# A new order of work on every engine in the attention phase of a cross-attention and FFN kernel

## What is computed

```python
def attn(q, k, v, wq, wk, wv, wo):          # q = layernorm(x), k = v = ctx
    Q, K, V = (split_heads(a @ w) for a, w in ((q, wq), (k, wk), (v, wv)))
    corr = irfft(rfft(Q) * conj(rfft(K)))   # over the 128 places
    top_vals, top_idx = top_k(corr, 4)
    w = softmax(top_vals)
    out = sum(w[i] * roll(V, top_idx[i]) for i in range(4))   # roll within a head's 16
    return merge_heads(out) @ wo

x = x + attn(layernorm(x), ctx, ctx, wq, wk, wv, wo)
x = x + ffn(layernorm(x), W_in, b_in, W_out, b_out)   # gelu, int8 weights, 16-bit activations
```

## Time and profile before

| | us |
|---|---|
| median of 3 runs | 1145.84 (1144.47 to 1146.34) |
| the profiled execution | 1144.86 |
| its span, first to last instruction | 1143.1 |
| TensorE busy | 1024.5 (90%) |
| VectorE busy | 970.0 (85%) |
| ScalarE busy | 942.9 (82%) |
| GpSimd busy | 518.1 (45%), nearly all of it in the attention phase |

### The profile page before, as it was taken

The page is one execution under the profiler, slowest core; times in us unless marked ns, Lnnn a source line. Parts: engine busy times, 40 slices in busy tenths (PEclk is TensorE's granted clock), DMA queues, the critical chain, the costliest instruction groups (busy, mean ns, idle before and its releaser), DMA issues. The chain is left out here.

```text
span 1143.1 us, 30275 instructions
## 1 busy us (share of the span) xinstructions
PE 1024.5 (90%) x9870; PEld 759.9 (66%) x9870; DVE 970.0 (85%) x2838; ACT 942.9 (82%) x1805; POOL 518.1 (45%) x742
## 2 busy tenths in 40 slices
PE   6888888888888888888888789999999999999998
PEld 5677666766667667667766654444444588888887
DVE  4777778777887777787777999999999899999998
ACT  4677877787788888777887778888888899999996
POOL 5887777777777777787777650000000100000000
PEclk9999999999999999999999999999999999999999
DMA  5443333223332433332333129999999999999995
GB/s 157 135 135 120 110 112 112 90 98 112 112 102 91 125 112 112 112 104 99 98 111 112 39 86 321 304 309 307 309 308 301 373 342 346 362 354 359 357 346 211
DMA packets 133783, 222.94 MB, mean 195 GB/s; under 512 B 72480, under 2 KB 76192, under 8 KB 129568
## 3 DMA queue, kind: packets, MB, share of 16 engines
q1 hardware_dynamic: 132272, 220.12, 56.8%
q10 hardware_dynamic: 1392, 1.31, 0.4%
HBM read 121.26 MB, written 83.89 MB: 179 GB/s over the span
## 5 line engine op out<-in xcount | busy, mean ns | idle before, releaser
L657 PE MATMUL sums<-wout,arena 128*128 128x256 f16 x2048 | 229.7, 273 | 1.2 <-DVE arena L1555 1.2
L657 PEld LDWEIGHTS sums<-wout,arena 128*128 128x128 f16 x2048 | 197.0, 98 | 32.4 <-DVE arena L1548 7.3
L1555 DVE SCALAR_TENSOR_TENSOR arena<-arena,wout_rel 128x512 f16<-128x512 int16 x256 | 180.2, 745 | 2.0 <-ACT arena L932 0.9
L477 PE MATMUL sums<-store_x,arena 128*128 128x256 f16 x768 | 94.1, 272 | 93.8 <-ACT arena L677 93.8
L748 ACT ACTIVATE arena<-arena 32x128 f32<-32x128 f32 x256 | 78.5, 307 | 118.5 <-DVE arena L1243 116.2
L1250 DVE SCALAR_TENSOR_TENSOR arena<-sums,arena 128x256 f32<-128x256 f32 x128 | 56.1, 480 | 130.5 <-ACT arena L716 130.5
L477 PEld LDWEIGHTS sums<-store_x,arena 128*128 128x128 f16 x768 | 70.7, 97 | 116.8 <-issue 108.9
L1021 POOL TENSOR_TENSOR arena<-arena 128x512 f16<-128x512 f32 x64 | 74.3, 1160 | 94.6 <-ACT arena L677 94.6
L626 PE MATMUL sums<-arena,win 128*128 128x512 f16 x512 | 115.9, 379 | 0.7 <-DVE arena L1500 0.7
L626 PE MATMUL bank<-arena,win 128*128 128x512 f16 x512 | 115.7, 379 | 0.0
L1519 DVE TENSOR_REDUCE hmax_all<-arena 128x1 f32<-128x1024 f32 x96 | 111.2, 1210 | 2.9 <-ACT arena L889 2.9
(11 more groups left out here) (152 smaller groups left out, 2428.2 us busy)
## 6 DMA issues: line engine op xcount, KB each, us to landing
hidden_scratch<-arena SPq DMA_DIRECT2D x32, 1536.0 KB, 5.6
arena<-hidden_scratch SPq DMA_DIRECT2D x64, 768.0 KB, 6.7
arena<-in_ctx_turned SPq DMA_DIRECT2D x64, 256.0 KB, 4.1
arena<-in_x_turned SPq DMA_DIRECT2D x64, 256.0 KB, 3.0
arena<-in_x SPq DMA_DIRECT2D x64, 256.0 KB, 3.9
x_scratch<-arena SPq DMA_DIRECT2D x64, 256.0 KB, 3.3
arena<-x_scratch SPq DMA_DIRECT2D x32, 512.0 KB, 6.0
out<-arena SPq DMA_DIRECT2D x31, 512.0 KB, 4.3
```

The lines of the kernel that those rows point to most:

```text
L477: last = nc.tensor.matmul(bank[1][:, b * D:(b + 1) * D], xt16[:, i, c, b * P:(b + 1) * P], w16[:, j, 0, c, :], start=c == 0 and k == 0, st ...
L657: last = nc.tensor.matmul(bank[m * 2 + k // 2][:, k % 2 * D:(k % 2 + 1) * D], gbuf[:, s, f, k * P:(k + 1) * P], wout16[:, f, :], start=f = ...
L1555: V.scalar_tensor_tensor(gbuf[:, 1, f, :], hq[:, f, :], wout_rel[:, f:f + 1], gbuf[:, 0, f, :], ALU.mult, ALU.subtract).then_inc(S["c_lo"], 1)
```

## The change

The code of every stage stays. What changes is the order of the calls on four engines.

- VectorE: `top_values` comes first in a step, `one_hot`, `sum_ex` and the softmax steps up to `mask_sum` follow for the same pair (t - 3) instead of the pair before (t - 4), then `mix_q`, then `spread_weights` and `turn_weights` for pair t - 3 instead of t - 4. `moments1` works on the pair whose statistics were just taken.
- ScalarE: `squares` moves ahead of `take_k`, `normalize2` behind `take_q_half`, `exponent` between `take_k` and `take_v`. `spread_blocks` remains the first call, for pair t - 4.
- GpSimd: `take_shift` ahead of `scale_both`.
- SyncE: context and x are loaded in step t for pair t + 1, ahead of them nothing but the previous step's loads; `store_x1` is issued for pair t - 6 instead of t - 7.
- The tails of these engines are rewritten to match.

The core of the diff. The tails are left out; their rows are the same stages in a changed order, with the softmax of a pair one place earlier:

```diff
@@ SyncE @@
             def step(t):
-                if active(t, 7):
-                    store_x1(t - 7)
-                if active(t, 0) and t >= X_FIRST:
-                    load_x(t)
-                if active(t, 0) and t > 0:
-                    load_turned(t)
-                if active(t, 0) and t > 0:
+                load_turned(t + 1)
+                if t > 0:
                     load_x_turned(t)
-                if 0 < t < X_FIRST:
-                    load_x(t)
+                if active(t, 6):
+                    store_x1(t - 6)
+                load_x(t + 1)
@@ ScalarE @@
                 if active(t, 4):
                     spread_blocks(t - 4)
+                if active(t, 6):
+                    squares(t - 6)
                 if active(t, 1):
                     take_k(t - 1)
+                if active(t, 3):
+                    exponent(t - 3)
+                if active(t, 1):
                     take_v(t - 1)
-                if active(t, 7):
-                    normalize2(t - 7)
                 if active(t, 0):
                     high_ct(t)
...
-                if active(t, 3):
-                    exponent(t - 3)
                 if active(t, 1):
                     take_q_half(t - 1)
-                if active(t, 6):
-                    squares(t - 6)
+                if active(t, 7):
+                    normalize2(t - 7)
                 if active(t, 0):
                     high_xt(t)
@@ GpSimd @@
-                scale_both(t - 7)
                 if active(t, 3):
                     take_shift(t - 3)
+                scale_both(t - 7)
                 if active(t, 2):
                     add_terms(t - 2)
@@ VectorE @@
             def step(t):
-                if active(t, 4):
-                    weigh_hot(t - 4)
...
-                if active(t, 1):
-                    moments1(t - 1)
-                if active(t, 4):
-                    spread_weights(t - 4)
                 if active(t, 3):
                     top_values(t - 3)
-                if active(t, 4):
-                    turn_weights(t - 4)
                 if active(t, 2):
                     products(t - 2)
                 if active(t, 3):
                     top_places(t - 3)
                     head_lags(t - 3)
+                    one_hot(t - 3)
+                    sum_ex(t - 3)
+                    weigh_hot(t - 3)
+                    invert_sum(t - 3)
+                    sum_hot(t - 3)
+                    mask_sum(t - 3)
                 if active(t, 1):
                     mix_q(t - 1)
+                if active(t, 3):
+                    spread_weights(t - 3)
+                    turn_weights(t - 3)
                 if active(t, 0):
                     statistics1(t)
-                if active(t, 3):
-                    one_hot(t - 3)
+                    moments1(t)
+                if active(t, 5):
+                    residual(t - 5)
                 if active(t, 7):
                     magnitude(t - 7)
-                if active(t, 5):
-                    residual(t - 5)
-                if active(t, 3):
-                    sum_ex(t - 3)
```

More of the change, by code:

```diff
@@ L33 @@
 W_STEP = 10
-X_FIRST = 3
 AHEAD = 6
@@ L355, in _ @@
                 step(t)
-            store_x1(PAIRS - 8)
-            load_x(PAIRS - 1)
-            load_turned(PAIRS - 1)
+            load_x_turned(PAIRS - 1)
             store_x1(PAIRS - 7)
-            load_x_turned(PAIRS - 1)
             store_x1(PAIRS - 6)
@@ L843, in _ @@
                 step(t)
+            squares(PAIRS - 7)
             take_k(PAIRS - 2)
-            normalize2(PAIRS - 8)
             exponent(PAIRS - 4)
+            take_v(PAIRS - 2)
             high_ct(PAIRS - 1)
-            take_v(PAIRS - 2)
             take_q_half(PAIRS - 2)
-            squares(PAIRS - 7)
             high_xt(PAIRS - 1)
@@ L854, in _ @@
             spread_blocks(PAIRS - 5)
+            normalize2(PAIRS - 8)
             take_q_half(PAIRS - 1)
+            squares(PAIRS - 6)
             exponent(PAIRS - 3)
@@ L860, in _ @@
             take_q(PAIRS - 1)
-            squares(PAIRS - 6)
             spread_blocks(PAIRS - 4)
@@ L1057, in _ @@
             scale_both(PAIRS - 8)
+            low_ot(PAIRS - 6)
             take_shift(PAIRS - 4)
-            low_ot(PAIRS - 6)
             add_terms(PAIRS - 3)
@@ L1344, in step @@
             def step(t):
-                if active(t, 4):
-                    weigh_hot(t - 4)
-                if active(t, 4):
-                    invert_sum(t - 4)
-                    sum_hot(t - 4)
-                    mask_sum(t - 4)
-                if active(t, 1):
-                    moments1(t - 1)
-                if active(t, 4):
-                    spread_weights(t - 4)
                 if active(t, 3):
                     top_values(t - 3)
-                if active(t, 4):
-                    turn_weights(t - 4)
                 if active(t, 2):
@@ L1386, in _ @@
                 step(t)
-            weigh_hot(PAIRS - 5)
-            invert_sum(PAIRS - 5)
-            sum_hot(PAIRS - 5)
-            mask_sum(PAIRS - 5)
-            moments1(PAIRS - 2)
-            spread_weights(PAIRS - 5)
             top_values(PAIRS - 4)
@@ L1395, in _ @@
             top_places(PAIRS - 4)
-            mix_q(PAIRS - 2)
-            magnitude(PAIRS - 8)
-            sum_ex(PAIRS - 4)
-            head_lags(PAIRS - 4)
-            statistics1(PAIRS - 1)
-            one_hot(PAIRS - 4)
-            turn_weights(PAIRS - 5)
-            moments1(PAIRS - 1)
+            statistics1(PAIRS - 1)
+            moments1(PAIRS - 1)
+            head_lags(PAIRS - 4)
+            one_hot(PAIRS - 4)
+            sum_ex(PAIRS - 4)
+            weigh_hot(PAIRS - 4)
+            invert_sum(PAIRS - 4)
+            sum_hot(PAIRS - 4)
+            mask_sum(PAIRS - 4)
+            mix_q(PAIRS - 2)
+            spread_weights(PAIRS - 4)
+            turn_weights(PAIRS - 4)
             residual(PAIRS - 6)
-            invert_sum(PAIRS - 4)
-            weigh_hot(PAIRS - 4)
-            sum_hot(PAIRS - 4)
+            products(PAIRS - 2)
             top_values(PAIRS - 3)
             mix_q(PAIRS - 1)
-            products(PAIRS - 2)
+            magnitude(PAIRS - 8)
             top_places(PAIRS - 3)
-            mask_sum(PAIRS - 4)
+            head_lags(PAIRS - 3)
+            one_hot(PAIRS - 3)
             sum_ex(PAIRS - 3)
-            head_lags(PAIRS - 3)
-            spread_weights(PAIRS - 4)
-            one_hot(PAIRS - 3)
+            weigh_hot(PAIRS - 3)
             invert_sum(PAIRS - 3)
-            weigh_hot(PAIRS - 3)
-            turn_weights(PAIRS - 4)
             sum_hot(PAIRS - 3)
```

## The result

The changed kernel takes **1073.14 us** (median of 4, 1071.59 to 1076.67) against 1145.43 (1144.47 to 1146.34) for the kernel before on the same chip: a ratio of 0.9373, 95% interval 0.9347 to 0.9399. The forecast was 1073.

What follows compares the result with a forecast made beforehand. A 10.03 us ScalarE-VectorE ring was taken to bound attention. First four steps 33.2, 55 x 8.68 = 477.4 and weights 10.6 make 521.2 against 594.3, a gain of 73.1: 1072.7, rounded to 1073 us; range 1062 to 1098.

Steps and rivals of the forecast that it cites:

- the old ring: Attention step before: VectorE's mix_q to turn_weights and ScalarE's spread_blocks to take_q_half wait in turn, 10.03 us a step.
- D: Rival: spread_blocks still ends up waiting for turn_weights, so the time stays as before, 1146 us; chance 0.02.
- The new ring: Attention step after, between ScalarE and TensorE, project_q through attend, take_q, squares and take_k: 8.68 us, kept 8.5 to 8.82.
- The sister ring through `transform`: Attention step after: take_q starts at most 1.35 us behind transform's start, giving a step of at most 8.82 us.
- VectorE's order at nothing: Attention steps: VectorE needs 8.25 us, 8.6 with FFN weights, both under the new step, so its reorder costs nothing.
- take_shift at nothing: GpSimd's step: take_shift ahead of scale_both costs nothing and takes 1.5 us from the path of exponent.
- The loads at nothing, -2 to +1: SyncE's earlier context and x loads and x1 store: costed at nothing, from -2 to +1 us.
- C: Rival: single context buffer; decides from a landing of 7.1 us, slower than before beyond 8.6; chance 0.04.
- Ahead of pair 2, 0 +- 1.5: Start of the kernel: order changes but each engine does the same work, put at 0 +- 1.5 us.
- Behind pair 61, 0 +- 1.5: End of attention: VectorE does one pair's softmax less after the last two mix_q, put at 0 +- 1.5 us.
- A, contention: Rival: VectorE stretched 0.88 us a step beside GpSimd, needing 9.13, so 1097 us; chance 0.07.
- B, squares waiting for minus_mean2: Rival: ScalarE's squares waits for GpSimd, holding take_k and project_q; step 9.1, 1096 us; chance 0.12.

Runs made afterwards that it cites:

- take_q_more: The changed kernel with one more 256-column copy into a spare tile in take_q on ScalarE: 1094.32 us.
- high_ct_more: The changed kernel with one more 256-column copy into a spare tile ahead of high_ct on ScalarE: 1074.69 us.
- vector_alone: The kernel before with the new VectorE order (step and tail) and nothing else: 1109.85 us.
- weights_aside: The changed kernel with ScalarE's FFN weight operation moved from behind take_q to behind high_ct: 1063.02 us.
- squares_behind: The changed kernel with squares behind take_q_half and ScalarE's FFN weight operation behind high_ct: 1055.21 us.
- loads_gpsimd_back: The changed kernel with SyncE's and GpSimd's old order: 1078.98 us.
- tail_spread: The changed kernel with spread_blocks of pair 59 moved ahead of take_q of pair 62 in ScalarE's tail: 1073.48 us.
- vector_exponent_shift: The kernel before with VectorE's new order, exponent ahead of take_v on ScalarE, and take_shift ahead of scale_both on GpSimd: 1068.66 us.
- The last kernel: squares_behind with, in ScalarE's tail, spread_blocks of 59 ahead of take_q of 62 and normalize2 of 56 ahead of take_k of 63: 1051.91 us.
- scalar_alone: The kernel before with the new order in ScalarE's step alone, its tail and all other engines as before: 1188.81 us.

## Why the prediction was right, point by point

**What bounds the kernel before.** Right. VectorE's order alone removes the wait of `spread_blocks`, and the old ring with it. D is out.

**The new ring.** Right, term by term:

| term | predicted | after |
|---|---|---|
| project_q to the end of attend | 3.68 | 3.68 |
| to high_ot | 0.05 | 0.03 |
| high_ot, take_ot | 1.10 | 1.12 |
| take_q | 0.84 | 0.83 |
| spread_blocks | 1.29 | 1.27 |
| squares | 0.98 | 1.00 |
| take_k | 0.60 | 0.57 |
| to project_q | 0.14 | 0.15 |
| step | 8.68 | 8.65 |

That these are the terms that count is shown by take_q_more against high_ct_more. TensorE's `project_q` starts 1.61 behind `project_v` (497.52 against 495.91) instead of 1.31, the 0.3 that the prediction names. The sister ring through `transform` wasn't reached, but only just. `transform` starts at 492.47; in vector_alone, where `take_q` waits for it, `take_q` starts 1.19 behind it, which here would be 493.66, and `take_q` starts at 493.70 behind `take_ot`. Both rings run through `take_q`, `spread_blocks`, `squares` and `take_k`, so the runs don't tell them apart.

**The FFN weights.** Right: 9.10 on average against 8.65 is 0.45, where 0.44 was predicted, and weights_aside gets back 10 us.

**VectorE's order at nothing.** Right for the changed kernel, but with little to spare. Of the two prices behind it, 8.6 is borne out by squares_behind, whose step is mostly 8.62 where VectorE carries FFN weights. That operation takes 0.32 from its start to the next (0.35 was predicted), so VectorE needs 8.30 without it, where 8.25 was predicted. In the changed kernel VectorE's rows of pairs 11 to 16 stand without a wait but one of 0.22, and `mix_q` comes every 8.62 there: it has 0.03 to spare against the ring.

**take_shift at nothing.** The number was right, the reason incomplete. In the changed kernel its old place costs nothing (loads_gpsimd_back keeps its step), but with `squares` off the path of `take_k` it is worth 28 us, 1097.11 against 1068.66. The prediction priced each part beside the finished whole; taken one after the other the same parts have other prices. VectorE's order gives 35 us, `exponent` 13 more, `take_shift` 28 more, and ScalarE's order on its own costs 44.

**The loads at nothing, -2 to +1.** Nearer to -4, as far as one run tells. `mix_ct` waits for the context 4.4 us in 2 steps instead of 8.7 in 6; with the old loads beside the other new orders it is 20.4 in 22, and loads_gpsimd_back is 4 us slower by its ratio (its four runs lie at 1074.5 to 1079.7, so this is hardly clear of noise). The prediction's condition, that a wait of GpSimd reaches the ring only if it outlasts GpSimd's spare time, is what the step of 11.3 us shows. No load of the context took over 4.5 to landing in the changed kernel, and C is out.

**The first four steps.** 34.67 instead of 33.2, at the upper bound of 34.7. One of them takes 9.45, with a granted clock of 0.95 in 30 to 65 us. squares_behind, whose order in these steps is the changed one's, has a granted clock of 1.00 there, takes 8.17 for that step, and 33.05 for the four.

**The sum.** The 55 steps took 551.45 - 64.76 = 486.69 where 477.4 + 10.6 = 488.0 was predicted, 1.3 less, and the first four 1.5 more. The two ends, -2.66 and +2.80, cancel as well. That the median came out at the very 1073 is luck; the step of 8.68 against 8.65 isn't.

**Ahead of pair 2, 0 +- 1.5.** Off by -2.66, and the runs don't put that down to the order. The windows of 15 to 30 us (length, busy us of TensorE, its weight loads, VectorE, ScalarE and GpSimd with counts, granted clock, DMA share, GB/s), of the kernel before, of the changed one, and of tail_spread, whose order there is the changed one's:

```profile
15.00:30.00 15.00, 11.44 (x139) 8.40 (x137) 10.00 (x28) 6.52 (x13) 10.51 (x14) 0.89 0.42 120
```
```profile
15.00:30.00 15.00, 11.36 (x152) 9.02 (x152) 10.74 (x36) 8.28 (x18) 11.99 (x16) 1.00 0.49 140
```
```profile
15.00:30.00 15.00, 11.76 (x141) 8.32 (x139) 8.56 (x23) 6.87 (x14) 10.32 (x14) 0.81 0.44 124
```

`mix_q` of pair 2 comes at 32.75, 30.09 and 32.80. The column to see is the granted clock: 0.89, 1.00, 0.81. Two executions of the same order, the last two, differ by 2.71 us here, the one at 2.4 GHz throughout, the other partly at 1.2, so a difference of 2.66 between single executions says nothing about the order. Nor is the clock all of it: vector_exponent_shift has 1.00 in this stretch, with ScalarE's and SyncE's old order at the start, and comes at 32.25.

**Behind pair 61, 0 +- 1.5.** Wrong by +2.8, and this is the term whose failure the runs explain: the work was counted (the softmax of one pair more), the waits were not. The FFN part stays, as predicted: from its first matmul to the end it takes 468.95 us before and 468.96 after. The difference lies ahead of it. From `mix_q` of 61 to that of 63 the kernel before takes 15.23, with 2.3 us of waits on VectorE, and the changed one 18.80, with 5.5; from there to the FFN it is 31.87 and 31.09. `turn_weights` of 60 must wait for `spread_blocks` of 59 to free its tile. In the loop that call always comes early enough; in the tail, written out by hand, it doesn't. tail_spread takes 1.3 us out between 61 and 63, and loses 1.1 again behind 63, at a granted clock of 0.89 instead of 0.95. The last kernel, with 3.11 of these waits left, has 516.45, close to before's 516.05.

**A, contention.** Out. `mix_q` takes 0.88 as before, and no row of the steady state is longer. That agrees with the rule cited in the prediction from the Trainium skill, page "SBUF — State Buffer", section "Who interferes with whom". The row of 1.65 at the start has both inputs in SBUF, which is not the case of the new neighbours; it is a single row, and no run here tests it.

**B, squares waiting for minus_mean2.** Out in the steady state: L746 starts at 495.80 without idle time, and `minus_mean2` (L964) ends at 495.01 + 0.22 = 495.23, so 0.57 is to spare, as the prediction found (0.6). In the tail it waits 0.9 once. The path itself exists: in loads_gpsimd_back, with GpSimd 2.59 us late, `squares` waits 2.00.

## What to carry to other kernels

When several engines each work through an order of their own, find the loop of calls that wait for each other, write its terms down from the rows, and ask of every call in it whether the dependence needs it or only the queue. The same operation cost 21 us on that loop and nothing measurable a few calls away. Redo this for each candidate order and do the prologue and the hand-written tail on their own: a part that is free in the finished order (`take_shift`) can be worth 28 us in a neighbouring one, and a tile that always comes free in time in the loop may not in the tail.

## What the hardware did that was not expected

TensorE's clock fell behind some waits of about 2 to 3 us, and such a wait is paid twice. In scalar_alone `project_q` waited 2.98 us and then took 2.55 us instead of 1.47, and the granted clock of that kernel is 0.96 over 60 to 300 us, a mean between stretches at 2.4 GHz and some at 1.2. Undisturbed steps with a wait of 2.02 at the same place ran at 2.4 GHz, as did the kernel before with 1.5. But in the same kernel another wait of 2.03 was followed by slow rows, and that step took 11.6 us:

```profile
440.94 1.73 PE L477 MATMUL sums<-store_x,arena 128*128 128x256 f16 x12 [2.03 <-ACT arena L677]
442.46 2.76 PE L534 MATMUL sums<-store_x,arena 128*128 128x256 f16 x12
```

In tail_spread `attend` waited 1.90 us at 586.33, and `project_out` behind it took 2.77 instead of 1.47:

```profile
586.33 1.22 PE L513 MATMUL bank<-arena,store_x 128*128 128x128 f32 x8 [1.90 <-ACT arena L740]
587.34 2.77 PE L526 MATMUL sums<-store_x,arena 128*128 128x256 f16 x12
```

So about 2 us of waiting was seen both with and without a fall; what decides, these runs don't settle. An order that leaves TensorE a wait of 2 us or more a step can thus be slower than its ring: scalar_alone was by some 15 us.
